# Gated attention: state update and chunk outputs as three single-pass products of high and low parts, and gate weights loaded in place

## What is computed

```python
def _gla_chunk(q, k, v, gf):          # q, k: 32 wide, v = x: 512 wide
    Bc = jnp.cumsum(gc, axis=2)       # gates, summed within a chunk of 64
    def step(S, inp):
        qh, kh, vh, Bh = inp
        Blast = Bh[:, -1, :]
        D = Bh[:, :, None, :] - Bh[:, None, :, :]
        A = jnp.where(tril, jnp.einsum('bid,bjd,bijd->bij', qh, kh, jnp.exp(D)), 0.0)
        o_intra = jnp.einsum('bij,bjv->biv', A, vh)
        o_inter = jnp.einsum('bid,bdv->biv', qh * jnp.exp(Bh), S)
        kd = kh * jnp.exp(Blast[:, None, :] - Bh)
        S_new = S * jnp.exp(Blast)[..., None] + jnp.einsum('bjd,bjv->bdv', kd, vh)
        return (S_new, o_intra + o_inter)
o = _gla_chunk(softmax(x @ Wq.T), sigmoid(x @ Wk.T), x, log_sigmoid(-k))
go = o @ Wog.T + x @ Wig.T
o = o * lax.rsqrt(jnp.mean(o * o, axis=-1, keepdims=True) + EPS) * g_norm_w * (go * sigmoid(go))
out = o @ Wo.T
```

## Time and profile before

| | |
|---|---|
| median of 3 runs | 962.32 us (961.0 to 963.45) |
| own time of the profiled execution | 961.3 us |
| its span, first to last instruction | 959.3 us |
| PE busy | 918.3 us, 96% of the span |
| DVE, ACT, POOL busy | 648.4, 400.2, 302.2 us |
| mean granted TensorE clock | 0.988 of full speed |
| gated attention | from 553 to some 760 us of the span |

### The profile page before, as it was taken

How to read it: one execution, slowest core, us unless ns; L and a number is a source line. 1 busy time by engine, 2 the same in 40 slices (tenths; PEclk the granted TensorE clock), 3 DMA queues, 4 the chain that set the end, 5 groups by cost and what they waited for, 6 DMA issues and landing times.

```text
span 959.3 us, 13818 instructions
## 1 busy us (share of the span) xinstructions
PE 918.3 (96%) x4964; PEld 719.2 (75%) x4964; DVE 648.4 (68%) x1268; ACT 400.2 (42%) x674; POOL 302.2 (32%) x270
## 2 busy tenths in 40 slices
PE   8999999997999999999998999999999999999994
PEld 6777877885787877876776767687867878878883
DVE  5766763577967688688766866866688887454413
...
GB/s 280 175 95 120 40 33 35 78 12 89 45 33 1 1 0 1 1 1 1 1 45 1 0 99 1 1 44 1 60 30 24 132 164 118 64 128 45 153 66 44
DMA packets 43973, 54.20 MB, mean 56 GB/s; under 512 B 6113, under 2 KB 25858, under 8 KB 43906
## 3 DMA queue, kind: packets, MB, share of 16 engines
...
...
## 4 chain that ended last, share of the span: by engine, by line
PE 58%; DVE 10%; issue 3%; ACT 3%; POOL 1%; DVEq 0%; ACTq 0%; POOLq 0%
PE ps_gla L41 14%; PE ps_gla L43 13%; PE ps_gla L42 13%; DVE acc L1606 6%; PE ps_gla L2192 6%; PE ps_gla L2193 5%; PE ps_gla L2292 1%; ACT acc L1324 1%; PE ps_gla L2278 1%; ACT fjunk L864 1%; PE ps_gla L2222 1%; PE ps_gla L2304 1%; PE ps_gla L2285 1%; DVE x L878 0%; POOL mh_lo L2156 0%
## 5 line engine op out<-in xcount | busy, mean ns | idle before, releaser
L1606 DVE SCALAR_TENSOR_TENSOR acc<-ps_gla,gu_scale,acc 128x512 f32<-128x512 f32 x264 | 196.9, 749 | 72.8 <-ACT acc L1324 50.2
L2192 PE MATMUL ps_gla<-xt_hi,gu_val 128*128 128x512 f32 x352 | 145.2, 412 | 11.1 <-PEq L71 4.7
L2193 PE MATMUL ps_gla<-xt_lo,gu_val 128*128 128x512 f32 x352 | 138.8, 394 | 0.0
L1324 ACT ACTIVATE acc<-ps_gla,gu_scale 128x512 f32<-128x512 f32 x88 | 60.6, 688 | 112.3 <-PE ps_gla L2193 112.3
L2192 PEld LDWEIGHTS ps_gla<-xt_hi,gu_val 128*128 128x128 f32 x352 | 66.9, 190 | 47.0 <-DVE acc L1606 28.2
L2099 POOL TENSOR_TENSOR fsg<-fsg,acc 128x512 f32<-128x512 f32 x44 | 62.4, 1418 | 123.5 <-DVE acc L1606 123.5
L657 POOL TENSOR_TENSOR a_rstd<-a_var,minus_half 128x1 f32<-128x1 f32 x16 | 10.6, 661 | 211.9 <-DVE a_var L538 211.9
L2193 PEld LDWEIGHTS ps_gla<-xt_lo,gu_val 128*128 128x128 f32 x352 | 67.1, 191 | 11.5
L2104 POOL TENSOR_TENSOR fh_lo<-fsg,fh_hi 128x512 fp32r<-128x512 f32 x44 | 57.3, 1303 | 46.8 <-ACT fh_hi L1336 46.8
L41 PE MATMUL ps_gla<-dn_hi,fh_hi 128*128 128x512 f32 x176 | 69.3, 394 | 0.0
L42 PE MATMUL ps_gla<-dn_hi,fh_lo 128*128 128x512 f32 x176 | 68.7, 390 | 0.0
...
## 6 DMA issues: line engine op xcount, KB each, us to landing
...
```

Of the source, the lines that this page charges most:

```text
L1324: act.activation(acc[part][u // 2 % 2][:, :], ps[:, FG, :], ACT.Copy, scale=gu_scale[:, part * IT + j, 0:1]).then_inc(s_g0, 1)
L1606: dve.scalar_tensor_tensor(out=a[:, :], in0=ps[:, FG + c, :], scalar=gu_scale[:, part * IT + j, c:c + 1], in1=a[:, :], op0=ALU.mult, op1=A ...
L2192: pe.matmul(ps[:, FG + c, :], gu_val[:, o, c, :], xt_hi[b % 2][:, c, :], start=True, stop=False)
L2193: pe.matmul(ps[:, FG + c, :], gu_val[:, o, c, :], xt_lo[b % 2][:, c, :], start=False, stop=True).then_inc(s_gu, 1)
```

## The change

`k_end` is made in two steps: a small product of keys and decay in `qx` (`key_ends`), a copy of it, repeated, as high part `k_hi` on ACT (`key_high`), and `k_lo` on DVE (`key_low`). Each tile of x is split into `x_part_hi` (ACT, `x_part_high`) and `x_part_lo` (DVE, `x_part_low`), in two buffers by turns; both for tile t + 1 stand in the queues at the end of tile t. The masked scores are split into `gat_hi` (ACT, `scores_high`) and `gat_lo` (DVE, `scores_low`). `update` and the first matmul of `outputs` become three products each. `update` waits for `s_xpl` too, `outputs` for `s_atl` in place of `s_at`. WIG, WOG and WO are loaded where their low parts will lie, and the loads wait for what lay there: WIG for one more up group, WOG for the last down product. The old raw buffer's place at 64 takes the parts of x.

```diff
--- before.py
+++ after.py
@@ -960,7 +960,7 @@
         f_junk = put("fjunk", [P, C], 186)
 
         w_at = [(188, 190), (94, 86), (76, 108), (116, 124)]
-        w_raw = [put("gw_qk_raw", [P, KC, P], 192)] + [put("gw_raw", [P, KC, C], 64)] * 2 + [put("gwo_raw", [P, KC, C], 124)]
+        w_raw = [put("gw_qk_raw", [P, KC, P], 192)] + [put(f"gw_raw{i}", [P, KC, C], w_at[i][1]) for i in (WIG, WOG, WO)]
         w_hi = [put(f"gw_hi{i}", [P, KC, w_cols[i]], w_at[i][0], F32R) for i in range(NW)]
         w_lo = [put(f"gw_lo{i}", [P, KC, w_cols[i]], w_at[i][1], F32R) for i in range(NW)]
         o_hi = put("o_hi", [P, KC, BLK], 132, F32R)
@@ -969,10 +969,15 @@
         p_hi = put("p_hi", [P, KC, BLK], 168, F32R)
         p_lo = put("p_lo", [P, KC, BLK], 176, F32R)
         q_state = put("q_state", [P, TB, REP, DK], 72)
-        k_end = put("k_end", [P, TB, REP, DK], 74)
+        k_hi = put("k_hi", [P, TB, REP, DK], 74, F32R)
+        k_lo = put("k_lo", [P, TB, REP, DK], 194, F32R)
+        x_part_hi = [put(f"x_part_hi{i}", [P, C], 64 + 2 * i, F32R) for i in range(2)]
+        x_part_lo = [put(f"x_part_lo{i}", [P, C], 68 + 2 * i, F32R) for i in range(2)]
         pair_t = [put(f"pair_t{i}", [2 * DK, 2, P], 84 + i) for i in range(2)]
         q_parts = [put(f"q_parts{i}", [P, P], 102 + i / 2, F32R) for i in range(2)]
         at = [put(f"gat{i}", [P, P], 103 + i / 2) for i in range(2)]
+        at_hi = [put(f"gat_hi{i}", [P, P], 196 + i / 2, F32R) for i in range(2)]
+        at_lo = [put(f"gat_lo{i}", [P, P], 103 + i / 2, F32R) for i in range(2)]
         state = [put(f"state{i}", [P, C], 104 + 2 * i) for i in range(2)]
         s_parts = [put(f"s_parts{i}", [P, C], 148 + 2 * i, F32R) for i in range(2)]
         o_tok = put("o_tok", [P, C], 184)
@@ -1241,11 +1252,10 @@
             sp.dma_start(b1_sb[:, :], b1).then_inc(m_b1, 16)
             for j in range(SCALES, IT):
                 down_scale(j)
-            sp.wait_ge(s_gu, KC * (unit(LAST, 3, 0) + 1))
+            sp.wait_ge(s_gu, KC * (unit(LAST, 3, 1) + 1))
             sp.dma_start(w_raw[WIG][:, :, :], wigT).then_inc(s_w[WIG], 16)
-            sp.wait_ge(s_wl, 2)
+            sp.wait_ge(s_dn, IT * NBLK)
             sp.dma_start(w_raw[WOG][:, :, :], wogT).then_inc(s_w[WOG], 16)
-            sp.wait_ge(s_dn, IT * NBLK)
             sp.dma_start(w_raw[WO][:, :, :], woT).then_inc(s_w[WO], 16)
             sp.dma_start(rw_sb[:, :], router_w.to_broadcast([P, C])).then_inc(s_rw, 16)
 
@@ -1378,6 +1388,25 @@
                     act.wait_ge(s_o, i - 1)
                 act.activation(q_parts[t % 2][:, :], ps[:, F, 2 * P:3 * P], ACT.Copy).then_inc(s_qh, 1)
 
+            def x_part_high(n, t):
+                i = TB * n + t
+                if i >= 2:
+                    act.wait_ge(s_o, i - 1)
+                act.wait_ge(rows.s_out, TB * n + t + 1)
+                act.activation(x_part_hi[t % 2][:, :], x[n][:, t, :], ACT.Copy).then_inc(s_xph, 1)
+
+            def scores_high(n, t):
+                i = TB * n + t
+                act.wait_ge(s_at, i + 1)
+                if i >= 2:
+                    act.wait_ge(s_o, i - 1)
+                act.activation(at_hi[t % 2][:, :], at[t % 2][:, :], ACT.Copy).then_inc(s_ath, 1)
+
+            def key_high(n):
+                act.wait_ge(s_kf, n + 1)
+                act.wait_ge(s_su, TB * n)
+                act.activation(k_hi[:, :, :, :], qx[:, :, :].unsqueeze(2).to_broadcast([P, TB, REP, DK]), ACT.Copy).then_inc(s_kh, 1)
+
             def state_high(n, t):
                 i = TB * n + t
                 act.wait_ge(s_s, i + 1)
@@ -1493,6 +1522,10 @@
                         softplus(0)
                     if b and j == 3:
                         rows.squares(act, b - 1, range(TB))
+                    if b == LAST and j == FRONT_SUMS + 2:
+                        key_high(0)
+                    if b == LAST and j == IT - 1:
+                        x_part_high(0, 0)
                     if b == 2 and j == 4:
                         weight_high(WQK)
             f_high(IT * NBLK - 1)
@@ -1507,6 +1540,7 @@
                     if n == 0 or t:
                         take_pairs(n, t)
                     take_queries(n, t)
+                    scores_high(n, t)
                     if 0 < n < LAST:
                         x_high(NBLK + n + 1, t)
                     elif n == LAST and t in (1, 2):
@@ -1524,6 +1558,8 @@
                     if t:
                         o_high(n, t - 1)
                     take_o(n, t)
+                    if n < LAST or t + 1 < TB:
+                        x_part_high(n + (t + 1) // TB, (t + 1) % TB)
                     if n == LAST and t == 1:
                         pair_weights(0)
                 if n < LAST:
@@ -1542,6 +1578,8 @@
                 if n == 0:
                     fold_norm_w(range(2, KC))
                 silu(n, 2)
+                if n < LAST:
+                    key_high(n + 1)
                 if n == 2:
                     take_scores(0, O)
                 p_high(n, 2)
@@ -1654,14 +1692,19 @@
             def query_copies(n):
                 dve.tensor_tensor(q_state[:, :, :, :], copies(qs[:, :, :]), copies(decay[:, 2, :, :]), ALU.mult)
 
-            def key_copies(n):
-                dve.tensor_tensor(k_end[:, :, :, :], copies(ks[:, :, :]), copies(decay[:, 3, :, :]), ALU.mult).then_inc(s_ft, 1)
+            def key_ends(n):
+                dve.wait_ge(s_qn, 3 * n + 3)
+                dve.tensor_tensor(qx[:, :, :], ks[:, :, :], decay[:, 3, :, :], ALU.mult).then_inc(s_kf, 1)
+
+            def key_low(n):
+                dve.wait_ge(s_kh, n + 1)
+                dve.tensor_tensor(k_lo[:, :, :, :], copies(qx[:, :, :]), k_hi[:, :, :, :].bitcast(F32), ALU.subtract).then_inc(s_ft, 1)
 
             def features(n):
                 key_pairs(n)
                 query_pairs(n)
+                key_ends(n)
                 query_copies(n)
-                key_copies(n)
 
             def q_low(n, t):
                 i = TB * n + t
@@ -1680,6 +1723,16 @@
                 if n:
                     dve.wait_ge(s_pl, KC * n - 1)
                 dve.tensor_tensor(at[t % 2][:, :], ps[:, A, 0:P], const.upto[:, :], ALU.mult).then_inc(s_at, 1)
+
+            def scores_low(n, t):
+                i = TB * n + t
+                dve.wait_ge(s_ath, i + 1)
+                dve.tensor_tensor(at_lo[t % 2][:, :], at[t % 2][:, :], at_hi[t % 2][:, :].bitcast(F32), ALU.subtract).then_inc(s_atl, 1)
+
+            def x_part_low(n, t):
+                i = TB * n + t
+                dve.wait_ge(s_xph, i + 1)
+                dve.tensor_tensor(x_part_lo[t % 2][:, :], x[n][:, t, :], x_part_hi[t % 2][:, :].bitcast(F32), ALU.subtract).then_inc(s_xpl, 1)
 
             def next_state(n, t):
                 i = TB * n + t
@@ -1876,6 +1930,7 @@
                     if b == LAST and j == FRONT_SUMS + 1:
                         key_pairs(0)
                     if b == LAST and j == FRONT_SUMS + 2:
+                        key_ends(0)
                         query_copies(0)
                     groups(b, j, 1)
                     if b == 0:
@@ -1896,9 +1951,10 @@
                         dve.wait_ge(s_zero, 1)
                         query_pairs(0)
                     if b == LAST and j == FRONT_SUMS + 2:
-                        key_copies(0)
+                        key_low(0)
             for c in range(KC):
                 x_low(NBLK + 1, c)
+            x_part_low(0, 0)
             weight_low(WIG)
             for n in range(NBLK):
                 for t in range(TB):
@@ -1908,6 +1964,7 @@
                     if 0 < n < LAST:
                         x_low(NBLK + n + 1, t)
                     state_low(n, t)
+                    scores_low(n, t)
                     if n == 0 and t == 0:
                         rows.mean_square(dve, LAST)
                     if n == 0 and t == 1:
@@ -1923,6 +1980,8 @@
                         residual(n - 1, t)
                     if t:
                         o_low(n, t - 1)
+                    if n < LAST or t + 1 < TB:
+                        x_part_low(n + (t + 1) // TB, (t + 1) % TB)
                     if n == LAST:
                         rank(0, 2 + t)
                 if n:
@@ -1956,6 +2015,8 @@
                     router(2)
                 if n == 0:
                     folded_low(range(2, KC))
+                if n < LAST:
+                    key_low(n + 1)
                 gated(n, 2)
                 if n == 2:
                     for t in range(2):
@@ -2275,7 +2336,9 @@
                 pe.wait_ge(s_s, i)
                 if n == LAST and t == 0:
                     pe.wait_ge(s_sb, 1)
-                pe.matmul(ps[:, S, :], k_end[:, t, :, :].rearrange("p r d -> p (r d)"), x[n][:, t, :], start=True, stop=True).then_inc(s_su, 1)
+                pe.wait_ge(s_xpl, i + 1)
+                k_parts = [k[:, t, :, :].rearrange("p r d -> p (r d)") for k in (k_hi, k_lo)]
```

(6 more changed lines are left out.)

11 lines of the change are left out of this document (9 added, 2 removed).

## The result

The changed kernel takes **1000.15 us** (median of 4 runs, 999.16 to 1001.01), the kernel before beside it 962.38 (4 runs). The ratio is 1.0393, 95% interval 1.0375 to 1.0411: 3.9% slower. The profiled execution took 999.7 us with a span of 997.7, 38.4 more than in the earlier trace rows.

What follows compares the result with a forecast made beforehand. PE was taken to bound the gated attention stage, so any wait in its queue costs its full length. 961.3 + 28.9 (waits, port, block 3) + 6.8 (clock) + 1.0 for the median gave 998 us, range 978 to 1014.

Steps and rivals of the forecast that it cites:

- The saving: Three single-pass products for one fp32 product in 16 updates and 16 chunk outputs: 0.17 us less each, 5.4 in all.
- The update's wait: At three tile boundaries per block PE waits for x_part_lo: 14.7 us net, 15.5 with block 0's extra 0.8.
- The 0.8 more at block 0's first boundary: ACT, already late there behind four squares, gets two more copies in its queue: 0.8 us more lost.
- The port: POOL's join of o lengthens DVE's x_part_lo at second and third boundaries of blocks 0 and 2: 4 x 0.75 = 3.0 us.
- The chunk output's wait: Outputs at first tiles of blocks 1 to 3 and block 0's fourth wait for the scores' low half: together 5.5 us.
- The 0.5 of block 0's fourth tile: Only half the products stand ahead of that tile's chunk output, so it waits 0.5 us for the scores' low half.
- The keys' 0.2: At a block's end a small key product, ACT copy and DVE subtraction replace k_end: 0.2 us through the gated product.
- Block 3: DVE's chain with rank makes three tiles take 28.8 us instead of 19.6; 4.9 us more than already counted.
- The clock: PE's longer waits in the changed loops lower its clock: four times 1.7 us, 6.8 us.
- rival D: The clock falls in nearly every tile, 13.6 us instead of 6.8, DVE first losing more at the port: 1005 to 1020; chance 0.07.
- Rival B: Only the update waits; DVE's low halves come in time, port free, clock stays: 14.7 us, 977; chance 0.18.
- Rival C: At each tile's update x_part's halves are ready before PE arrives, so 5.4 us are gained: 957; chance 0.05.

Runs made afterwards that it cites:

- the filled run: The changed kernel with products that nothing reads put in PE's queue ahead of the update's wait: 992.44 us, ratio 1.0328.
- the loads alone: The kernel before with only the change's gate weight load addresses and SP waits: 962.35 us beside 961.93, ratio 1.0004.

## Why the prediction came out as it did

**The saving** (5.4 us): as sized. Three products 0.23 apart take 0.69 for 0.86, and the periods of the runs without these waits are shorter by 0.16 with the update's products alone (6.37) and 0.31 with both (6.22). By the four passes that the Trainium skill gives to true fp32 ("FP8 and Floating Point Precision", TensorE Precision Notes) an estimate would have been 0.21 and 0.43; the row was the better guide.

**The update's wait** (15.5): the mechanism held. The high half began 1.71 us after the chunk output (I had 1.62), the low half 2.36 (2.30), the update 3.20 (3.05). The tile period of block 1 is 7.78, I had 7.53: a net 1.25 where I took 1.0. The 0.8 more at block 0's first boundary was too much: in the filled run that period is 8.22, I had 8.62.

**The port** (3.0, and 1.5 inside block 3): 1.44 to 1.48 us in blocks 2 and 3, and in block 1 DVE was first, as expected. There the join pays: 1.73 us instead of 1.27, which nobody waits for. In block 0 it was 1.14, since the join had started earlier: 0.45 lost where 0.75 was sized. That the loser depends on who is first is what the Trainium skill says ("SBUF — State Buffer", Who interferes with whom). The trace agrees in these tiles: DVE loses in block 2, where it starts second, and POOL in block 1, where it does. The last section has two cases in which the starts shown don't tell.

**The chunk output's wait** (5.5): 5.9 us, 2.03, 1.68 and 1.35 at the first tiles of blocks 1 to 3. The 0.5 of block 0's fourth tile shows only in the filled run (0.51). The keys' 0.2 at a block's end can't be told apart in the changed kernel; in the run with the update alone and the halves in the gaps block 0's end is 0.3 longer than before (28.54 against 28.22) and the other two are not longer.

**Block 3** (28.8 for three tiles): 28.90 in the filled run, 30.16 with the clock.

**The clock** (4 x 1.7 = 6.8): the product was right by luck, since both factors were wrong. There were eight stretches, the count of rival D, and they cost 7.1 us, not its 13.6. So one costs 0.9 on average: 1.35 to 1.6 for two of the three in block 0 and both in block 2, 1.3 for the two in a row in block 3 together, and nothing for the last in blocks 0 and 3. Where it cost 1.5, a part of the slow time fell into the wait; where it cost nothing, another operand set the tile's end.

The sum without the clock was 28.9; the loops and ends give 7.2 + 3.7 + 5.1 + 9.3 + 4.5 = 29.8, taking blocks 0, 2 and 3 from the filled run. With the clock's 7.1 that is 36.9 against the forecast's 35.7. The 1.5 that lead to 38.4 lie outside the stage, almost all of them ahead of the first output (see the loads alone), and the prediction had no term for them.

**What the prediction did not see** is what lies under these waits. It read each term as a loss that would go with its wait. The runs show two more limits close behind the first: the output's operand just in time, and DVE's work plus its hole. In block 1 the period goes from 7.78 only to 7.22 when the wait of 1.26 is gone. Rival B, only the update waits (977), is not what limiting the change to the update gives: that costs 35 us, with the port and the clock in it, which B had left out. Rival C's condition, the high half ahead of o's copy, was tried: it gives 979, not 957, so it is not enough. Where the same operations were put in the two holes the loss was 0.23%. So of 37.8 us some 35.5 were the order and not the work. What remains is block 3, where DVE has little room (20.75 against 19.60 us), and block 0 with its end (18.24 and 29.34 against 17.43 and 28.22), where ACT's squares make the first boundary late; against them stand 1.2 us of saving in blocks 1 and 2.
